# Local attention with the heads' pairs in the two halves of TensorE, a new order of the period, and turns in the probabilities' banks

## Chip, cores and metric

The kernel runs on one core of one Trainium2 chip. The metric is the device time in microseconds of one execution; the time given is the median of several. A core has TensorE (PE in the profile, PEld its weight loads), VectorE (DVE), ScalarE (ACT), GpSimd (POOL) and SyncE (SP), each with a queue of its own that runs in order; they meet at semaphores.

## What is computed

The whole reference is a chain of blocks (a state-space block, a mixture of experts, a windowed attention and a local-attention block of two layers). The change touches the last alone. Each of its two layers does, for 4096 tokens of 128 channels (16 sequences of 256):

```python
h = shift_token(x)
q, k, v = split(h @ wqkv)              # 8 heads of 64
q, k = rotary_xpos(l2norm(q) * qs, l2norm(k) * ksc)
sim = 8.0 * q @ k.T                    # windows of 64, each with the window before it
attn = softmax(where(mask, -max, sim))
x = x + (attn @ v) @ wo
x = x + feed_forward(layernorm(shift_token(x)))
```

## The kernel before

`phase_local` has one instruction stream for each engine, written out by hand. Each layer n has an attention stage of NB passes b, and each pass two chunks c = 0, 1 of 128 tokens. A number i = 2b + c counts chunks. Chunk 0 of a pass holds two windows whose keys lie in the same 128 tokens; chunk 1 also takes the 64 keys before each window. The 8 heads of a chunk are taken in two units u of four heads (HU = 4, U = 4 units in a pass).

The stages of a chunk, and who does them:

- `project` (L2620, PE): queries and keys into the two banks of `qk_ps`; `project_v` (L2625): values into the one bank `a_ps`.
- `rotary` (L3041 to L3043, DVE): three products with the tables, out of PSUM, into `c1` and `c2`. Their sum is made by DVE for keys (`rotary_sum`, L3048) and by POOL for queries (L2552).
- `square` (ACT, L2880) and `square_sums` (DVE, L3054); `query_norms` and `key_norms` (POOL, L2563 and L2573) take the power -1/2.
- `scale_k` (L3060, DVE) puts the norm into the keys; queries get theirs in the exponentials.
- `turn_q`, `turn_k` (L2633, L2641, PE): transposes, back into `qk_ps`; `q_copy` and `k_copy` (ACT, L2903) take them to SBUF. `kT` has two halves: in each only the 64 rows of one head of a pair are filled and the others stay zero, so that a product over all 128 rows gives one head. `qT` has both heads of a pair in its 128 rows.
- `scores` (PE): a bf16 product that writes the mask (L2654), then the products (L2658 for c = 0, L2663 for c = 1) on top of it, for one unit in one bank `s_ps[u % 2]`.
- `maxima` (DVE, L3070 and L3074): the row maxima and the exponentials' bias. `exps` (ACT, L2913): one instruction a head. `divide` (DVE, L3081 and L3084): the probabilities `pn`.
- `transpose_p` (PE, L2674) into `t_ps`, `p_copy` (ACT, L2922), `weigh` (PE, L2694 for c = 0, L2702 for c = 1) into `o_ps`, `o_copy` (ACT, L2928), `output` (PE, L2711) into `a_ps`, `residual` (DVE, L3090), which adds `a_ps` to the stream R.
- `transpose_r` (PE, L2612) turns R of a pass into `a_ps`, and `shift` (ACT) makes `hT` of it.

The functions `attend` of the four engines give the order of a pass: the chunks of pass b are scored while those of pass b + 1 are projected, and the last units of pass b - 1 are weighed. `first` and `last` leave out what the ends lack. `a_ps` is used in turn by output, the value projection and the transposes of R. After the attention stage come 8 groups of feed-forward.

Of the kernel before, what the change touches and what calls it, by code (L numbers as in the profile page):

```python
# [2419 lines left out]
def phase_local(nc, t, old, r_dram, x3_dram, out_dram):  # L2420
# [13 lines left out]
    with ExitStack() as ctx:  # L2434
# [8 lines left out]
        c1, c2 = ([m.sb(f"{n}{i}", [P, NH, HD]) for i in range(2)] for n in ("c1", "c2"))  # L2443
        qT = [m.sb(f"qT{i}", [P, NP, T]) for i in range(2)]
        kT = [m.sb(f"kT{i}", [P, 2, NP, T]) for i in range(2)]
        v = [m.sb(f"v{i}", [P, NCH, INNER]) for i in range(3)]
        near = [m.sb(f"near{i}", [P, INNER]) for i in range(2)]
        top, nbias = m.sb("top", [P, HU]), m.sb("nbias", [P, 2, HU])
# [21 lines left out]
        s_ps = [m.ps(f"s{i}") for i in range(2)]  # L2470
        t_ps = [m.ps(f"t{i}") for i in range(2)]
        ft_ps = qk_ps[:, Q, :]
        h_ps = s_ps + t_ps
# [10 lines left out]
        CLEARED = 5  # L2484
        near_in = m.sem("near_in")
        NW = 16 * len(t.sources)

        with nc.Block() as block:  # L2488
# [50 lines left out]
            def _(pool):  # L2539
# [5 lines left out]
                for i in range(2):  # L2545
                    nc.gpsimd.memset(kT[i][:, :, :, :], 0.0).then_inc(cleared, 1)

                def rotary_sum(l, b, c):

                    i = NCH * b + c  # L2550
                    pool.wait_ge(l.rot_rd[Q], i + 1)
                    nc.gpsimd.tensor_tensor(c1[Q][:, :, :], c1[Q][:, :, :], c2[Q][:, :, :], ALU.add).then_inc(l.sum_rd[Q], 1)  # L2552
# [30 lines left out]
                for n in range(2):  # L2583
                    for b in range(NB):
                        for c in range(NCH):
                            if b == 0:
                                key_norms(at[n], b, c)
                                rotary_sum(at[n], b, c)
                                query_norms(at[n], b, c)
                                if n == 0 and c == 0:  # L2590
                                    clear(pool, old)
                            else:
                                rotary_sum(at[n], b, c)
                                query_norms(at[n], b, c)
                                key_norms(at[n], b, c)
# [8 lines left out]
            def _(pe):  # L2604
# [10 lines left out]
                def project(n, b, c, x):  # L2615
# [3 lines left out]
                    at_least(pe, l.xT_sb[x], (x + 1) * i)  # L2619
# [8 lines left out]
                def turn_q(n, b, c):  # L2628
                    l, i = at[n], NCH * b + c
                    pe.wait_ge(l.sum_rd[Q], i + 1)  # L2630
                    pe.wait_ge(l.sq_rd[Q], i + 1)
                    for j in range(NP):
                        last = pe.transpose(qk_ps[:, Q, j * P:(j + 1) * P],  # L2633
                                            c1[Q][:, 2 * j:2 * j + 2, :].rearrange("p h d -> p (h d)"), ident[:, :])
                    last.then_inc(l.xT_mm[Q], 1)

                def turn_k(n, b, c):
                    l = at[n]
                    pe.wait_ge(l.kn_rd, NCH * b + c + 1)
                    for j in range(NP):  # L2640
                        last = pe.transpose(qk_ps[:, K, j * P:(j + 1) * P],  # L2641
                                            c1[K][:, 2 * j:2 * j + 2, :].rearrange("p h d -> p (h d)"), ident[:, :])
                    last.then_inc(l.xT_mm[K], 1)

                def scores(n, b, u):

                    l, p, c, d = at[n], b % 2, u // NU, u % NU
                    i = U * b + u
                    if d == 0:
                        pe.wait_ge(l.xT_sb[Q], NCH * b + c + 1)  # L2650
                        pe.wait_ge(l.xT_sb[K], 2 * (NCH * b + c + 1))
                    at_least(pe, l.ex_rd, HU * (i - 1))
                    bank = s_ps[u % 2][:, :].rearrange("p (h k) -> p h k", h=HU)
                    pe.matmul(bank, identb[:, :], mask[:, c, :, :], start=True, stop=False, skip_group_check=True)  # L2654
                    for k in range(2):
                        j = 2 * d + k
                        if c == 0:
                            last = pe.matmul(bank[:, 2 * k:2 * k + 2, :], qT[p][:, j, 0:P], kT[p][:, :, j, 0:P],  # L2658
                                             start=False, stop=True, skip_group_check=True)
                        else:  # L2660
                            for r in range(2):
                                q0 = P + r * HD
                                last = pe.matmul(bank[r * HD:(r + 1) * HD, 2 * k:2 * k + 2, :], qT[p][:, j, q0:q0 + HD],  # L2663
                                                 kT[p][:, :, j, q0 - HD:q0 + HD], start=False, stop=True, skip_group_check=True)
                    last.then_inc(l.s_mm, 1)

                def transpose_p(n, b, u):
# [4 lines left out]
                    at_least(pe, l.pT_sb, i - 1)  # L2672
                    for h in range(HU):
# [40 lines left out]
                def attend(n, b, first=False, last=0):  # L2714

                    l = at[n]
                    scores(n, b, 0)
                    if not first:
                        transpose_p(n, b - 1, U - 2)
                    if last < 2:  # L2720
                        project(n, b + 1, 0, Q)
                        if first:
                            pe.wait_ge(l.hT_sb, 2 * (b + 2))
                        else:
                            pe.wait_ge(l.res_rd, NCH * (b - 1))
                        project_v(n, b + 1, 0)
                    if not first:
                        weigh(n, b - 1, U - 2)

                    turn_k(n, b, 1)  # L2730
                    scores(n, b, 1)
                    if last < 2:
                        project(n, b + 1, 0, K)
                    if not first:
                        transpose_p(n, b - 1, U - 1)
                    if last < 2:
                        turn_q(n, b + 1, 0)
                    if not first:
                        if last < 2:
                            pe.wait_ge(l.v_sb, NCH * (b + 1) + 1)  # L2740
                        else:
                            pe.wait_ge(l.res_rd, NCH * (b - 1))
                        output(n, b - 1, 0)
                        weigh(n, b - 1, U - 1)

                    scores(n, b, 2)
                    transpose_p(n, b, 0)
                    if last < 2:
                        project(n, b + 1, 1, Q)
                        if first:  # L2750
                            pe.wait_ge(l.v_sb, NCH * (b + 1) + 1)
                        else:
                            pe.wait_ge(l.res_rd, NCH * (b - 1) + 1)
                        project_v(n, b + 1, 1)
                    weigh(n, b, 0)
                    if last < 1:
                        pe.wait_ge(l.v_sb, NCH * (b + 2))
                        transpose_r(n, b + 2)

                    if last < 2:  # L2760
                        turn_k(n, b + 1, 0)
                    scores(n, b, 3)
                    if last < 2:
                        project(n, b + 1, 1, K)
                    transpose_p(n, b, 1)
                    if last < 2:
                        turn_q(n, b + 1, 1)
                    if not first:
                        if last == 0:
                            pe.wait_ge(l.hT_sb, 2 * (b + 3))  # L2770
                        elif last == 1:
                            pe.wait_ge(l.v_sb, NCH * (b + 2))
                        else:
# [519 lines left out]
```

## Time and profile before

| | |
|---|---|
| median of 3 runs | 2178.75 us (2176.16 to 2181.96) |
| profiled execution, its own time | 2176.2 us |
| its span, first to last instruction | 2174.4 us |
| mean granted clock of TensorE | 0.929 |
| PE busy | 1781.2 us (82%) |
| DVE busy | 1635.1 us (75%) |
| ACT busy | 1271.2 us (58%) |
| POOL busy | 957.9 us (44%) |

The shares are means over the whole span. Of it, the local-attention block takes what lies behind 1297 us: an attention stage from there to 1649 us, feed-forward, and the same again for layer 2 from about 1730 to 2062 us. In the rows below, the three windows of layer 1 are its first pass, its 14 middle passes and its last pass up to the first feed-forward product. In a timeline, a start and the next start give what an instruction costs in a full queue; the duration is longer, since the end of one overlaps the next. An idle time in brackets is that before the instruction, with what ended it.

### The profile page before, as it was taken

The page shows a single profiled execution, that of the slowest core. Times are in us where ns is not written, and L with a number is a line of the kernel's source. Part 1 is how long each engine was busy: PE and PEld are TensorE (multiplying, and loading weights), DVE is VectorE, ACT ScalarE, POOL GpSimd, SP SyncE. Part 2 cuts the span into 40 slices and gives each one's busy share as a digit, 9 for nine tenths or more (in the row PEclk, how much of TensorE's full clock was granted, in tenths as well). Part 3 has the DMA queues.
Part 4 walks back from the last instruction along what each step waited for, and adds up shares of the span by engine and source line. Part 5 has one row for each costly group of instructions (what it writes and reads, how often), then busy time and mean ns, then how long its engine had stood idle before and what let it go on. Part 6 is the DMA issues. An engine that isn't in the chain of part 4 may idle for free. (4 is left out here: it accounts for less than half of the span.)

```text
span 2174.4 us, 36880 instructions
## 1 busy us (share of the span) xinstructions
PE 1781.2 (82%) x12448; PEld 976.1 (45%) x12448; DVE 1635.1 (75%) x3467; ACT 1271.2 (58%) x2737; POOL 957.9 (44%) x773
## 2 busy tenths in 40 slices
PE   5888898865889998859943757999998899999875
PEld 2333333332344444424423424655655556566543
DVE  5999999995577777622235767999986689999775
ACT  5777877740344444414434236888884388888721
POOL 5777887761012222223431245555550255555311
PEclk8999999996899999959976878999999999999997
DMA  5333333312111111114235140000001000000010
GB/s 150 110 111 119 122 108 116 93 49 81 39 37 36 41 36 44 31 41 133 65 105 165 52 137 15 16 21 16 11 16 23 13 16 21 16 16 11 15 42 23
DMA packets 107401, 125.47 MB, mean 58 GB/s; under 512 B 28804, under 2 KB 79151, under 8 KB 106224
## 3 DMA queue, kind: packets, MB, share of 16 engines
q1 hardware_dynamic: 103120, 115.07, 18.7%
q0 software_dynamic: 4096, 8.06, 1.1%
q8 instruction: 101, 1.65, 0.3%
q14 instruction: 84, 0.69, 0.1%
HBM read 71.60 MB, written 38.11 MB: 50 GB/s over the span
## 5 line engine op out<-in xcount | busy, mean ns | idle before, releaser
L394 POOL TENSOR_TENSOR m_bu<-m_dtu,m_brow 128x1024 f32<-128x1024 f32 x128 | 299.8, 2358 | 55.6 <-DVE m_hs L818 53.9
L818 DVE TENSOR_TENSOR_SCAN m_hs<-m_ps_da,m_bu 128x1024 f32<-128x1024 f32 x128 | 292.3, 2283 | 3.0 <-POOL m_bu L394 2.5
L1363 ACT ACTIVATE a_pt<-a_ps_s 128x1024 f32<-128x1024 f32 x128 | 131.1, 1024 | 226.7 <-PE a_ps_s L1141 226.7
L523 PE MATMUL m_ps_y_ps<-m_prod,m_ident 128*128 128x512 f32 x512 | 243.1, 597 | 0.0
L2913 ACT ACTIVATE l_pe<-l_ps_s,l_nbias,l_qs 128x128 f32<-128x128 f32 x512 | 227.9, 459 | 1.6
L1480 DVE TENSOR_REDUCE a_mpad<-a_ps_s 128x4 f32<-128x1024 f32 x128 | 156.9, 1226 | 92.3 <-PE a_ps_s L1133 91.1
L1133 PE MATMUL a_ps_s<-a_heads 32*128 32x256 f32 x1024 | 187.5, 446 | 43.6 <-DVE a_mpad L1480 28.5
L670 ACT ACTIVATE m_ps_da<-m_dt,m_a_neg 128x510 f32<-128x510 f32 x256 | 166.0, 681 | 74.3 <-DVE m_hs L818 73.4
L1141 PE MATMUL a_ps_s<-a_qm,a_heads 32*128 32x256 f32 x1024 | 184.7, 437 | 1.8 <-ACT a_pt L1363 1.4
L1067 POOL TENSOR_TENSOR a_rstd<-a_ve,a_mhalf 128x2 f32<-128x2 f32 x48 | 33.8, 705 | 303.0 <-DVE a_ve L1438 163.3
L828 DVE TENSOR_TENSOR m_prod<-m_hs,m_ps_c_ps 128x1024 f32<-128x1024 f32 x128 | 153.6, 1200 | 12.1 <-PE m_ps_c_ps L509 12.1
L2620 PE MATMUL l_ps_qk<-t_wqkv,l_hT 128*128 128x512 f32 x256 | 140.7, 634 | 9.4 <-ACT l_kT L2903 5.8
L523 PEld LDWEIGHTS m_ps_y_ps<-m_prod,m_ident 128*128 128x128 f32 x512 | 96.6, 192 | 108.7 <-issue 106.6
L3084 DVE TENSOR_TENSOR l_pn<-l_pe,l_ri 128x512 f32<-128x512 f32 x128 | 138.6, 1082 | 4.4
L1133 PEld LDWEIGHTS a_ps_s<-a_heads 32*128 32x128 f32 x1024 | 82.2, 193 | 129.6 <-PE a_ps_s L1141 60.1
L2552 POOL TENSOR_TENSOR l_c<-l_c 128x512 f32<-128x512 f32 x64 | 103.9, 1623 | 42.4 <-DVE l_c L3043 42.4
L3070 DVE TENSOR_REDUCE l_top<-l_ps_s 128x4 f32<-128x512 f32 x128 | 88.2, 689 | 35.9 <-PE l_ps_s L2658 23.8
L509 PE MATMUL m_ps_c_ps<-m_bc,m_sel 96*128 96x512 bf16 x128 | 49.1, 383 | 76.4 <-DVE m_prod L828 69.3
L3041 DVE TENSOR_TENSOR l_c<-l_ps_qk,t_tab 128x512 f32<-128x512 f32 x128 | 87.9, 686 | 29.9 <-PE l_ps_qk L2620 29.8
L2563 POOL TENSOR_TENSOR l_qs<-l_sc,l_mhalf 128x8 f32<-128x8 f32 x64 | 106.6, 1666 | 5.3
L2573 POOL TENSOR_TENSOR l_rink<-l_sc,l_mhalf 128x8 f32<-128x8 f32 x64 | 106.6, 1665 | 5.4
L2913 ACT ACTIVATION_READ_ACCUMULATOR l_pe<-l_ps_s,l_nbias,l_qs 128x1 f32 x512 | 105.0, 205 | 0.0
(339 smaller groups left out, 4252.1 us busy)
## 6 DMA issues: line engine op xcount, KB each, us to landing
m_brow<-state_rows SPq DMA_DIRECT2D x64, 512.0 KB, 4.3
slots<-m_void SPq DMA_DIRECT2D x16, 516.0 KB, 5.4
l_near<-l_v SPq DMA_DIRECT2D x64, 128.0 KB, 2.3
e_xs<-slots SPq DMA_DIRECT2D x16, 258.0 KB, 2.8
ys<-m_void SPq DMA_DIRECT2D x8, 512.0 KB, 5.3
qk<-a_qk SPq DMA_DIRECT2D x16, 256.0 KB, 2.0
a_heads<-qk SPq DMA_DIRECT2D x64, 64.0 KB
ew_w<-in_w SPq DMA_DIRECT2D x2, 2048.0 KB, 11.8
```

The costliest lines, as they stand in the source:

```text
L394: nc.gpsimd.tensor_tensor(bu[s % 4][:, :, :], dtu[p][:, :, :], b2, ALU.mult).then_inc(bu_rd, 1)
L523: last = pe.matmul(y_ps[:, h, :], ident[:, :], prod[d % 3][:, h, :], start=False, stop=(s == NS - 1))
L670: last = nc.scalar.activation(da[s % 2][:, h, :, 1:], dt[p][:, h, :, 1:], ACT.Exp, scale=a_neg[:, h, s:s + 1])
L818: dve.tensor_tensor_scan(hs[s % 4][:, :, :].rearrange("p h t -> p (h t)"), da[s % 2][:, :, :, :].rearrange("p h q t -> p (h q t)"), bu[s % ...
L828: dve.tensor_tensor(prod[d % 3][:, :, :], hs[s % 4][:, :, :], c2, ALU.mult).then_inc(prod_rd, 1)
L1133: last = pe.matmul(dst[:, j, :], qT[p][r, g, c * P:(c + 1) * P], kT[p][r, g, :], start=True, stop=True)
L1141: last = pe.matmul(s2[:, j, :], kT[p][r, g, c * P:(c + 1) * P], qm[p][r, g, :], start=True, stop=True)
L1363: nc.scalar.activation(pt[t % 2][:, :, :], s2[:, :, :], ACT.Exp).then_inc(exp_rd, 1)
L1480: dve.tensor_reduce(dst, src[:, :, :], AX.X, ALU.max, negate=True).then_inc(max_rd, 1)
L2620: pe.matmul(qk_ps[:, x, :], hT[b % 2][:, c * P:(c + 1) * P], t.wqkv[n][:, x * INNER:(x + 1) * INNER], start=True, stop=True).then_inc(l.x_ ...
L2913: nc.scalar.activation(pe_[u % 2][:, h, :], s_ps[u % 2][:, h * P:(h + 1) * P], ACT.Exp, bias=nbias[:, u % 2, h:h + 1], scale=qs[b % 2][:, ...
L3084: dve.tensor_tensor(pn[u % 2][:, :, :], pe_[u % 2][:, :, :], ri[:, :].unsqueeze(2).to_broadcast([P, HU, P]), ALU.mult).then_inc(l.pn_rd, 1)
```

## The change

1. *Scores.* `kT` loses its zero halves: it holds both heads of a pair in its 128 rows, like `qT`. A score product now contracts 64 rows, those of one head, r = 0 or 1. Heads with r = 0 write bank 0 of `s_ps`, those with r = 1 bank 1. All 8 heads of a chunk are scored at once; there is one set of two banks. Chunk 1 has products of 64 rows by 64 columns. `maxima` is one reduce over both banks, and `k_copy` one copy.
2. *Turns.* From chunk 2 (queries) or 1 (keys) on, `turn_q` and `turn_k` write into `t_ps[1]` and `t_ps[0]`, the banks of the transposed probabilities, with waits for their copies; `project` waits for the rotary and the squares of the chunk before. `c1` gets two buffers.
3. *Order.* The `attend` of each engine is now one body for a chunk. TensorE: scores; the turn of R (c = 1); probabilities; both projections; probabilities; output; weigh; turn_k; project_v; weigh; turn_q.
4. *GpSimd.* The sum of the queries' rotary waits for `kn_rd`, the scaling of the keys of the chunk before. The key norm comes ahead of the query norm. The memsets of `kT` go.

```diff
+        kept = {Q: 2, K: 1}
+
+        def turned(i, x):
+            return qk_ps[:, x, :] if i < kept[x] else t_ps[1 - x][:, :]
...
                 def rotary_sum(l, b, c):
 
                     i = NCH * b + c
                     pool.wait_ge(l.rot_rd[Q], i + 1)
+                    if i > 1:
+                        pool.wait_ge(l.kn_rd, i)
...
+                    for r in range(2):
+                        pe.matmul(bank[r], identb[:, :], mask[:, c, :, :], start=True, stop=False, skip_group_check=True)
+                    for j in range(NP):
                         if c == 0:
+                            for r in range(2):
+                                last = pe.matmul(bank[r][:, j, :], qT[p][side[r], j, 0:P], kT[p][side[r], j, 0:P],
+                                                 start=False, stop=True, skip_group_check=True)
                         else:
+                            for q in range(2):
+                                q0 = P + q * HD
+                                for r in range(2):
+                                    last = pe.matmul(bank[r][side[q], j, :], qT[p][side[r], j, q0:q0 + HD],
+                                                     kT[p][side[r], j, q0 - HD:q0 + HD], start=False, stop=True,
+                                                     skip_group_check=True)
```

The new order of TensorE and of VectorE:

```diff
                 def attend(n, b, first=False, last=0):
 
                     l = at[n]
+                    for c in range(NCH):
+                        scores(n, b, c)
+                        before = (b, 0) if c == 1 else (b - 1, 1)
+                        behind = not first or c == 1
+                        if c == 1 and last < 1:
+                            pe.wait_ge(l.v_sb, NCH * (b + 1) + 1)
+                            transpose_r(n, b + 2)
+                        if behind:
+                            transpose_p(n, before[0], NU * before[1])
                         if last < 2:
+                            project(n, b + 1, c, Q)
+                            project(n, b + 1, c, K)
+                        if behind:
+                            transpose_p(n, before[0], NU * before[1] + 1)
+                        if not first:
+                            if c == 0:
+                                pe.wait_ge(l.v_sb, NCH * (b + 1))
+                            elif last == 0:
+                                pe.wait_ge(l.hT_sb, 2 * (b + 3))
+                            elif last == 1:
+                                pe.wait_ge(l.v_sb, NCH * (b + 1) + 1)
+                            else:
+                                pe.wait_ge(l.res_rd, NCH * (b - 1) + 1)
+                            output(n, b - 1, c)
+                        if behind:
+                            weigh(n, before[0], NU * before[1])
+                        if c == 0:
+                            turn_k(n, b, 1)
+                        elif last < 2:
+                            turn_k(n, b + 1, 0)
+                        if last < 2:
+                            if not first:
+                                pe.wait_ge(l.res_rd, NCH * (b - 1) + c + 1)
+                            else:
+                                pe.wait_ge(l.hT_sb, 2 * (b + 2 + c))
+                            project_v(n, b + 1, c)
+                        if behind:
+                            weigh(n, before[0], NU * before[1] + 1)
+                        if last < 2:
+                            turn_q(n, b + 1, c)
...
                 def attend(n, b, first=False, last=0):
+                    for c in range(NCH):
+                        summed = (b, 1) if c == 0 and not first else (b + 1, 0) if c == 1 and last < 2 else None
+                        if summed:
+                            square_sums(n, *summed, K)
+                        maxima(n, b, c)
+                        if summed:
+                            square_sums(n, *summed, Q)
+                        if last < 2:
+                            rotary(n, b + 1, c, Q)
+                        if c == 0:
+                            scale_k(n, b, 1)
+                        elif last < 2:
+                            scale_k(n, b + 1, 0)
+                        else:
+                            norm_stats(n, 0)
+                        if last < 2:
+                            rotary(n, b + 1, c, K)
+                            rotary_sum(n, b + 1, c, K)
+                        divide(n, b, NU * c)
+                        if not first:
+                            residual(n, b - 1, c)
+                        divide(n, b, NU * c + 1)
```

ScalarE's order: shift (c = 1), p_copy, all exps of the chunk, p_copy, k_copy, both squares, v_copy, o_copy, q_copy.

## Rows read from the trace of the kernel before

**Rows 1.** Windows of layer 1: length, PE, PEld, DVE, ACT, POOL busy, clock, DMA.
```profile
1323.71:1343.14 19.43, 16.08 (x86) 8.59 (x86) 16.66 (x34) 15.26 (x46) 9.01 (x8) 1.00 0.06 14
1343.14:1627.49 284.35, 269.65 (x1932) 170.51 (x1930) 262.31 (x534) 246.39 (x727) 152.84 (x140) 1.00 0.07 16
1627.49:1648.98 21.49, 16.26 (x158) 12.18 (x156) 11.23 (x36) 14.46 (x48) 2.91 (x3) 0.92 0.04 10
```

**Rows 2.** VectorE's timeline in one pass: start us, duration us, engine, line.
```profile
1449.57 0.69 DVE L3070 TENSOR_REDUCE l_top<-l_ps_s 128x4 f32<-128x512 f32 x1 [0.15 <-PE l_ps_s L2658]
...
1450.38 0.69 DVE L3054 TENSOR_REDUCE l_ss<-l_sq 128x8 f32<-128x512 f32 x1
1450.98 0.68 DVE L3041 TENSOR_TENSOR l_c<-l_ps_qk,t_tab 128x512 f32<-128x512 f32 x1
...
1452.36 0.69 DVE L3048 TENSOR_TENSOR l_c<-l_c 128x512 f32<-128x512 f32 x1
1452.97 0.28 DVE L3090 TENSOR_TENSOR t_r<-l_ps_a,t_r 128x128 f32<-128x128 f32 x1
...
1453.98 0.68 DVE L3054 TENSOR_REDUCE l_ss<-l_sq 128x8 f32<-128x512 f32 x1
...
1456.05 0.69 DVE L3041 TENSOR_TENSOR l_c<-l_ps_qk,t_tab 128x512 f32<-128x512 f32 x1 [0.55 <-PE l_ps_qk L2620]
...
1457.32 0.68 DVE L3060 TENSOR_TENSOR l_c<-l_c,l_rink 128x512 f32<-128x512 f32 x1
...
1458.13 1.55 DVE L3084 TENSOR_TENSOR l_pn<-l_pe,l_ri 128x512 f32<-128x512 f32 x1
1459.99 0.69 DVE L3070 TENSOR_REDUCE l_top<-l_ps_s 128x4 f32<-128x512 f32 x1 [0.31 <-PE l_ps_s L2663]
```

**Rows 3.** TensorE's timeline in the same pass; the tile of the array behind MATMUL.
```profile
1452.55 0.34 PE L2702 MATMUL l_ps_o<-l_pT,l_near 128*64 128x64 f32 x4
...
1453.16 0.39 PE L2654 MATMUL l_ps_s<-t_mask,t_identb 128*128 128x512 bf16 x1
...
1454.99 1.02 PE L2620 MATMUL l_ps_qk<-t_wqkv,l_hT 128*128 128x512 f32 x2
1455.85 1.02 PE L2625 MATMUL l_ps_a<-t_wqkv,l_hT 128*128 128x512 f32 x2
1456.80 0.66 PE L2694 MATMUL l_ps_o<-l_pT,l_v 128*64 128x128 f32 x8
...
1458.06 0.66 PE L2641 MATMUL l_ps_qk<-t_ident,l_c 128*128 128x128 f32 x4
1458.55 0.38 PE L2654 MATMUL l_ps_s<-t_mask,t_identb 128*128 128x512 bf16 x1
1458.86 1.08 PE L2663 MATMUL l_ps_s<-l_kT,l_qT 128*64 128x256 f32 x8
```

**Rows 4.** GpSimd's timeline: a sum beside VectorE's scaling, and one beside other work.
```profile
1457.49 1.65 POOL L2552 TENSOR_TENSOR l_c<-l_c 128x512 f32<-128x512 f32 x1 [0.75 <-DVE l_c L3043]
...
1716.94 1.27 POOL L2552 TENSOR_TENSOR l_c<-l_c 128x512 f32<-128x512 f32 x1 [2.07 <-DVE l_c L3043]
```

**Rows 5.** TensorE's timeline in the windowed stage: products over 32 rows.
```profile
800.60 0.48 PE L1133 MATMUL a_ps_s<-a_heads 32*128 32x256 f32 x2
800.62 0.48 PE L1141 MATMUL a_ps_s<-a_qm,a_heads 32*128 32x256 f32 x2
```

**Rows 6.** One line's instructions: a reduce of 1024 elements, min/median/max ns.
```profile
L1480 DVE TENSOR_REDUCE a_mpad<-a_ps_s x128: 1218/1226/1227, 533.9 to 919.9; 128x4 f32<-128x1024 f32 x128
```

**Rows 7.** The page's part 5: the exponentials, busy us, mean ns, idle before.
```profile
L2913 ACT ACTIVATE l_pe<-l_ps_s,l_nbias,l_qs 128x128 f32<-128x128 f32 x512 | 227.9, 459 | 1.6
```

**Rows 8.** Windows where TensorE paused: columns as in the first group.
```profile
1627.60:1631.10 3.50, 1.44 (x22) 1.21 (x22) 2.12 (x5) 1.23 (x5) 1.91 (x2) 1.00 0.02 5
1631.10:1634.50 3.40, 3.40 (x13) 2.85 (x13) 0.94 (x3) 3.33 (x11) 0.00 (x0) 0.50 0.00 0
1651.60:1655.00 3.40, 1.94 (x6) 0.64 (x5) 2.93 (x14) 0.69 (x1) 1.11 (x1) 1.00 0.08 14
```

More of the change, by code:

```diff
@@ L2643, in turn_k, with scores @@
                     last.then_inc(l.xT_mm[K], 1)
[L2645 to L2656, printed above, removed]
+                def scores(n, b, c):
+                    l, p, i = at[n], b % 2, NCH * b + c
+                    pe.wait_ge(l.xT_sb[Q], i + 1)
+                    pe.wait_ge(l.xT_sb[K], i + 1)
+                    at_least(pe, l.ex_rd, NH * i)
+                    bank = [s_ps[:, r, :].rearrange("p (j t) -> p j t", j=NP) for r in range(2)]
+                    side = [slice(r * HD, (r + 1) * HD) for r in range(2)]
+                    for r in range(2):
+                        pe.matmul(bank[r], identb[:, :], mask[:, c, :, :], start=True, stop=False, skip_group_check=True)
+                    for j in range(NP):
@@ L2716, in attend @@
                     l = at[n]
[L2717 to L2738, printed above, removed]
-                        if last < 2:
[L2740 to L2773, printed above, removed]
-                            pe.wait_ge(l.res_rd, NCH * (b - 1) + 1)
-                        output(n, b - 1, 1)
@@ L2899, in k_copy @@
                     if c == 0:
[L2900 to L2904 removed]
+                        at_least(act, l.s_mm, NCH * (b - 1))
+                    nc.scalar.copy(kT[b % 2][:, :, c * P:(c + 1) * P],
+                                   turned(NCH * b + c, K).rearrange("p (j t) -> p j t", j=NP)).then_inc(l.xT_sb[K], 1)
                 def exps(n, b, u):
@@ L3092, in attend @@
                 def attend(n, b, first=False, last=0):
-                    if not first:
-                        divide(n, b - 1, U - 2)
-                        square_sums(n, b, 1, K)
-                    maxima(n, b, 0)
-                    if last < 2:
-                        rotary(n, b + 1, 0, Q)
-                    scale_k(n, b, 1)
-                    if not first:
-                        divide(n, b - 1, U - 1)
-                    maxima(n, b, 1)
-                    if last < 2:
-                        square_sums(n, b + 1, 0, Q)
-                        rotary(n, b + 1, 0, K)
-                        rotary_sum(n, b + 1, 0, K)
@@ L3108, in attend @@
-                    if not first:
-                        residual(n, b - 1, 0)
-                    divide(n, b, 0)
-                    if last < 2:
-                        square_sums(n, b + 1, 0, K)
-                    maxima(n, b, 2)
-                    if last < 2:
-                        rotary(n, b + 1, 1, Q)
-                        scale_k(n, b + 1, 0)
-                    else:
-                        norm_stats(n, 0)
-                    divide(n, b, 1)
-                    maxima(n, b, 3)
@@ L3123, in attend @@
-                    if last < 2:
-                        square_sums(n, b + 1, 1, Q)
-                        rotary(n, b + 1, 1, K)
-                        rotary_sum(n, b + 1, 1, K)
-                    if not first:
-                        residual(n, b - 1, 1)
+                    for c in range(NCH):
+                        summed = (b, 1) if c == 0 and not first else (b + 1, 0) if c == 1 and last < 2 else None
[4 more added lines that the diff above has]
+                            square_sums(n, *summed, Q)
+                        if last < 2:
+                            rotary(n, b + 1, c, Q)
+                        if c == 0:
+                            scale_k(n, b, 1)
+                        elif last < 2:
+                            scale_k(n, b + 1, 0)
+                        else:
+                            norm_stats(n, 0)
+                        if last < 2:
+                            rotary(n, b + 1, c, K)
[4 more added lines that the diff above has]
+                        divide(n, b, NU * c + 1)
```

147 lines of the change are left out of this document (66 added, 81 removed).

## Prediction

> **What bounds the kernel now.** I read the stage windows first. They cut layer 1's attention into its first pass (b = 0), the 14 middle passes and the last one [rows 1]: 284.35 us for 28 chunks of 128 tokens, 10.155 us a chunk, with TensorE busy 269.65 us (95%), VectorE 262.31 (92%), ScalarE 246.39 (87%) and the granted clock at 1.00. So three engines are nearly full, TensorE first, and no long wait is left; a change must shorten the work of both TensorE and VectorE to gain, and must not make them wait for each other. Layer 2 runs the same code and I take the same numbers for it.
>
> Then the timelines of VectorE [rows 2] and TensorE [rows 3] over one pass, for start-to-start costs (a duration overlaps the next instruction by about 0.09 us). The reader should see that VectorE's rows are back to back, and that there is one long L3084, 1.55 us instead of 0.69, which ends 0.54 us after GpSimd's sum at 1457.49 + 1.65 [rows 4].
>
> **What the change does to the work of a chunk.**
> - TensorE, scores. Before, a chunk of c = 0 is two units of four passes over 256 columns (0.86 each, as the two 512-column passes of a projection take [rows 3]), and one of c = 1 two units of 1.02. Now head pairs sit in the two 64-row halves of the array. That such row groups run side by side is shown by another stage: four matmuls on four groups of 32 rows start within 0.02 us [rows 5], where one after the other would start 0.21 apart (256 columns, half of a 512-column pass). [...] Per pair of chunks 3.8 becomes 2.0: 0.9 us less a chunk, and TensorE's 9.6 us becomes 8.7.
> - VectorE. Two maxima with their bias (0.81 each, 1449.57 to 1450.38) become one of 1024 elements. The same form takes 1.23 elsewhere [rows 6], so 1.35 with the bias: 0.27 less. GpSimd's sum now starts behind the scaling of the keys and lies beside the keys' rotary, which reads PSUM: the 0.87 of the long L3084 goes. 9.37 becomes 8.2.
> - ScalarE: one key copy over 128 partitions for two over 64. Eight exps remain, 8 x 0.46 = 3.7 us [rows 7]. It falls below 8.8 a chunk.
> - The turns now go to the probabilities' banks (`turned`), so a projection waits for the rotary and the squares of the chunk before and not for the copy of its turn. Both lie a slot back, so it has long been met and adds nothing.
> - The memsets of kT and their two signals only ran before the first chunk, beside loads and a projection on the slow clock: nothing.
>
> By work alone a chunk would cost 8.7 (TensorE) and not 10.155. But the orders are new, so I followed the waits around one chunk.
>
> **The loop that closes.** All of a_ps is one bank. Its users in a chunk i are the output of chunk i-2, the residual on VectorE that reads it, and then `project_v` of chunk i+2. In the new order `project_v` waits for that residual of the same slot, and VectorE's slot is: maxima, query sum of squares, rotary Q, scale_k, rotary K, its sum, divide, residual. Maxima waits for the scores of the slot. Behind `project_v` stand weigh and turn_q, then the next scores. So in every slot with a projection:
>
> scores -> maxima ... residual -> project_v -> weigh -> turn_q -> next scores.
>
> Its length, step by step:
> - scores to maxima: a first mask (one bf16 pass of 512 columns, half of an fp32 pass, 0.22), a second with the change of tile (0.31), matmul to maxima 1.13 (1458.86 to 1459.99), and 0.05 for a wider first weight load: 1.71 [rows 2, 3].
> - VectorE, maxima to residual: 1.35 + 0.60 (sum of squares, 1450.38 to 1450.98) + 1.27 (rotary Q, 1456.05 to 1457.32) + 0.60 (scale_k) + 1.38 (rotary K, 1450.98 to 1452.36) + 0.61 (its sum) + divide and residual 1.01 + 0.08 (one after the other, 1452.97 to 1453.98, and the end of the last) = 6.90 [rows 2].
> - the signal to TensorE: 0.06, estimated from the small gaps.
> - project_v 0.95, weigh 0.61, turn_q 0.49 (as turn_k, 1458.06 to 1458.55): 2.05 [rows 3].
>
> Sum 10.7 us (10.64 to 10.71 by chunk; I take 10.67), against 10.155. The residual used to be waited for one chunk later and so never closed a loop: now three engines have less to do and each chunk is 0.5 us longer. Over 28 chunks of two layers: 56 x 0.515 = +28.8 us.
>
> Other waits fit within it. The scores have one pair of banks now, so the next scores need all exps of the chunk: these end 1.4 + 3.7 us behind the start of maxima, and maxima to the next scores is 9.0. The last turn of probabilities (0.5), its copy (0.6) and the key copy follow them and are done by about 6.5. The key norm is ready before scale_k, since its sum of squares now comes before maxima. GpSimd's sum starts about 4.1 us behind maxima and takes 1.27 when nothing of VectorE disturbs it, 1.65 beside scale_k [rows 4]. At 1.27 it ends 5.4 behind; the keys' sum, held like that L3084 until 0.54 after it, then ends at 5.9, when it would anyway (5.20 + 0.69). At 1.65 it adds up to 0.4 to the loop (56 x 0.4 = +22). I take nothing, because the instructions beside it read PSUM.
>
> **The two ends.** In the first pass there is no residual to wait for. Its two slots are set by exps, key copy or pT copy, weigh and turn_q: about 8.2 us each, so 16 for 19.43 [rows 1], 3.4 less. The last pass has no projections: 1.4 + 3.7 + copy 0.6 + scores 1.7 = about 7.8 from scores to scores, then the last exps, one divide, norm, turns: about 17.4 for 21.49, 4.1 less. Two layers: -15 us, an estimate.
>
> Without any other effect: +28.8 - 15 = +14 us.
>
> **The clock.** TensorE now waits for the residual in each slot, 10.67 - 8.7 = 2 us, unevenly: about 2.2 in c = 0, 1.6 in c = 1, where the residual stream is transposed as well. [...] I expect falls in some slots: 12 in 56, with 0 and 28 (every c = 0) as bounds. A fall comes just as the wait ends, when all of TensorE's work is in the loop: 3.4 us at half speed lose up to 1.7; I take 1.6. 12 x 1.6 = +19 us; bounds 0 and +45.
>
> [...]
>
> [...]
>
> **Sum.** The profiled execution took 2176.2 us (span 2174.4, 1.8 around it), the median is 2178.75. 2176.2 + 14 + 19 = 2209; on the median 2212.
>
> **Rivals.**
> 1. *The work decides* (faster). If the loop had slack somewhere that I misread, a chunk falls to TensorE's 8.7: 56 x 1.45 = -81, with the ends -15: 2083. The point from which it decides is a loop under 10.4 us (below that the ends outweigh it). For it: all three engines lose work. Against it: every term of the 10.67 is a measured row and the waits are in the code.
> 2. *The loop without falls of the clock*: 2178.75 + 14 = 2193. It is the low side of my own case.
> 3. *The 64-row halves don't overlap*, or the small matmuls of c = 1 are issued too slowly: scores take another 0.9 to 1.7 us, all of it in the loop: 56 x 0.9 = +50 and more, 2262. Against it: rows 5, though those are 32-row groups. A fall in each c = 0 slot gives about 2238, and with GpSimd at 1.65 again 2260.
> 4. *The same*: a loop of 10.4, 0.27 shorter than mine, cancels the ends: 2179.
>
> **Chances.** The residual loop at about 10.7 with or without falls of the clock, 2187 to 2242: 0.66. Rival 3, 2242 to 2285: 0.16. Same (within 0.3%, 6.5 us, about what this measurement can tell from nothing): 0.08. Faster: 0.10. Range 2180 to 2262; the likeliest case alone 2187 to 2242. Slower 0.82.
>
> **What would show it.** Of the changed kernel: L3084 never long; one reduce of about 1.23 us a chunk; the pairs of score matmuls starting within 0.02 us; 28 middle chunks of about 10.7 us (300 us a layer, more with falls); TensorE and VectorE under 85% there; and as the longest wait of the stage `project_v` on the residual, about 2 us, 56 times. The granted clock under 1.00 in the middle would show the falls. I am wrong if the wait for the residual is short or absent, or if a chunk takes under 10.2 us.

## The result, and the profile after

| | before | changed |
|---|---|---|
| median of 4 runs, us | 2177.45 (2175.56 to 2181.96) | 2241.74 (2236.8 to 2242.72) |
| profiled execution, us (span) | 2176.2 (2174.4) | 2242.72 (2240.9) |
| mean granted clock | 0.929 | 0.913 |

The ratio is 1.0289, with a 95% interval of 1.0271 to 1.0307: 2.9% slower. The rise was 64 us where 33 was forecast.

The stage windows of layer 1 in the changed kernel, cut as in [rows 1] from first maxima to first maxima (length, PE, PEld, DVE, ACT, POOL busy, clock, DMA):

```profile
1324.97:1342.31 17.34, 13.35 (x107) 7.63 (x108) 15.55 (x32) 14.31 (x47) 6.87 (x8) 1.00 0.02 4
1342.31:1660.03 317.72, 258.60 (x2267) 171.19 (x2268) 229.19 (x477) 230.02 (x698) 142.86 (x141) 0.95 0.07 15
1660.03:1681.47 21.44, 15.42 (x170) 12.55 (x171) 10.51 (x30) 13.14 (x43) 3.28 (x3) 0.84 0.04 10
```

Against [rows 1], the 14 middle passes have less work on each engine (TensorE 259 us for 270, VectorE 229 for 262, ScalarE 230 for 246) and take 33.4 us longer; in the second layer the same stretch takes 32.8 us longer. Those 66 us are the whole difference: the first passes give back 4.9 (2.1 and 2.8), the last passes nothing (+0.1 for both), and all else is 5.1 longer.

What TensorE waits for, in the view of waits of layer 1's middle passes (us in total, times, longest):

```profile
PEld l_ps_a L2635 <- DVE t_r L3079: 65.7, 28, 2.7
PE l_ps_a L2635 <- DVE t_r L3079: 59.0, 28, 2.4
```

This is `project_v` (L2635) on the residual (L3079), in every one of the 28 chunks: 59 us of 318, which is all of TensorE's idle time there (317.72 - 258.60 = 59.1). The loop can be walked in the timelines of one chunk without a fall of the clock. First VectorE, from maxima to the next maxima (start, duration):

```profile
1410.39 1.23 DVE L3058 TENSOR_REDUCE l_top<-l_ps_s 128x8 f32<-128x1024 f32 x1 [4.08 <-PE l_ps_s L2672]
...
1415.57 0.71 DVE L3038 TENSOR_TENSOR l_c<-l_c 128x512 f32<-128x512 f32 x1
1416.20 0.17 DVE L3070 RECIPROCAL l_ri<-l_rs 128x4 f32<-128x4 f32 x1
1416.40 0.69 DVE L3073 TENSOR_TENSOR l_pn<-l_pe,l_ri 128x512 f32<-128x512 f32 x1
1417.01 0.28 DVE L3079 TENSOR_TENSOR t_r<-l_ps_a,t_r 128x128 f32<-128x128 f32 x1
...
1421.21 1.22 DVE L3058 TENSOR_REDUCE l_top<-l_ps_s 128x8 f32<-128x1024 f32 x1 [2.51 <-PE l_ps_s L2678]
```

And TensorE's timeline from the end of that residual to the scores:

```profile
1417.35 1.13 PE L2635 MATMUL l_ps_a<-t_wqkv,l_hT 128*128 128x512 f32 x2 [2.17 <-DVE t_r L3079]
1418.40 0.34 PE L2723 MATMUL l_ps_o<-l_pT,l_near 128*64 128x64 f32 x4
...
1419.02 0.66 PE L2645 MATMUL l_ps_t<-t_ident,l_c 128*128 128x128 f32 x4
1419.51 0.59 PE L2668 MATMUL l_ps_s<-t_mask,t_identb 128*128 128x512 bf16 x2
1420.04 1.10 PE L2678 MATMUL l_ps_s<-l_kT,l_qT 64*64 64x128 f32 x32
```

VectorE needs 6.90 us from maxima to the end of the residual, TensorE 3.92 from there to the next maxima, 10.82 in all, and each waits while the other works: TensorE 2.17 us, VectorE 2.51. The divide ahead of the residual costs 0.81 (reciprocal and product, 1416.20 to 1417.01).

The fall of the clock, in three windows of 3.40 us:

```profile
1403.10:1406.50 3.40, 1.55 (x10) 0.71 (x10) 3.10 (x8) 2.47 (x7) 0.34 (x2) 1.00 0.01 2
1406.50:1409.90 3.40, 3.40 (x22) 2.37 (x20) 0.00 (x0) 1.38 (x3) 1.80 (x2) 0.50 0.35 77
1409.90:1413.30 3.40, 3.40 (x24) 2.27 (x21) 2.88 (x6) 2.04 (x8) 0.72 (x2) 1.00 0.01 2
```

TensorE was busy for 1.55 of 3.40 us around a wait for the residual (2.00 us, ending at 1404.95); in the next 3.40 the granted clock was 0.50 instead of 1.00. VectorE has no work at all in that window: all that is left of the loop is TensorE's part, as the prediction said, so the half speed goes straight into the slot. Such a slot takes 12.36 to 12.40 us, the others 10.81 to 10.86. There are nine in each layer's middle. Of the 16 distances between them 12 are 34.1 us, which is near to three slots of which one is drawn out (10.83 + 10.83 + 12.40 = 34.06); the others are 23.9 or 44.4 us. In layer 1 two slots hold another 0.24 and 0.34 us (11.06 and 12.73), which nothing here explains. So the middles come out as 56 x (10.83 - 10.155) + 18 x 1.57 = 37.8 + 28.3 = 66.1 us, where 66.2 was measured.

### The profile page after: what moved, and what is told of

Read it like the earlier page. It is cut to its first block and busy times, and to the rows that moved or that the text cites. A ratio compares the mean times of both kernels' runs of the same rounds, so it can differ in the third digit from the quotient of the medians.

```text
span 2240.9 us, 38370 instructions
## 1 busy us (share of the span) xinstructions
PE 1757.5 (78%) x13216; PEld 979.1 (44%) x13216; DVE 1561.0 (70%) x3339; ACT 1233.3 (55%) x2673; POOL 931.1 (42%) x771
## 5 line engine op out<-in xcount | busy, mean ns | idle before, releaser
L3058 DVE TENSOR_REDUCE l_top<-l_ps_s 128x8 f32<-128x1024 f32 x64 | 78.4, 1225 | 190.8 <-PE l_ps_s L2672 100.2
L2635 PE MATMUL l_ps_a<-t_wqkv,l_hT 128*128 128x512 f32 x128 | 72.3, 647 | 117.7 <-DVE t_r L3079 117.7
L2630 PE MATMUL l_ps_qk<-t_wqkv,l_hT 128*128 128x512 f32 x256 | 125.0, 610 | 0.8 <-ACT l_hT L2875 0.8
L2922 ACT COPY l_pT<-l_ps_t 128x512 f32<-128x512 f32 x128 | 76.7, 599 | 64.0 <-PE l_ps_t L2695 63.2
L2576 POOL TENSOR_SCALAR l_sc<-l_ss 128x8 f32<-128x8 f32 x64 | 15.4, 241 | 210.8 <-DVE l_ss L3044 210.8
```

Of the source, the lines that this page charges most:

```text
L2630: pe.matmul(qk_ps[:, x, :], hT[b % 2][:, c * P:(c + 1) * P], t.wqkv[n][:, x * INNER:(x + 1) * INNER], start=True, stop=True).then_inc(l.x_ ...
```

## The experiments

The runs were made on three chips. On two of them the kernel before takes 2215.5 and 2216.0 us, some 38 more. In the traces from these two the first maxima of layer 1 come at 1360 to 1370 us, in the others at 1324 to 1328, so nearly all of the difference lies ahead of the local attention. So ratios to the kernel before on the same chip are compared, or the length of layer 1's and 2's middle passes.

**The place of the residual.** The diagnosis is a loop through VectorE's queue. If it is right, what stands ahead of the residual counts in full, although the amount of work is unchanged. The first run puts one divide behind the residual, the second the keys' rotary and its sum as well.

```diff
     rotary(n, b + 1, c, K)
     rotary_sum(n, b + 1, c, K)
+    residual(n, b - 1, c)
     divide(n, b, NU * c)
-    residual(n, b - 1, c)
     divide(n, b, NU * c + 1)
```

```diff
+    residual(n, b - 1, c)
     rotary(n, b + 1, c, K)
     rotary_sum(n, b + 1, c, K)
     divide(n, b, NU * c)
-    residual(n, b - 1, c)
     divide(n, b, NU * c + 1)
```

> The changed kernel with one edit: VectorE makes the residual ahead of the first divide instead of behind it. Theory (the residual loop sets the slot): the loop loses one divide, 0.81 us, so a middle chunk takes 10.02 instead of 10.83 us, TensorE's wait for the residual falls from 2.2 to about 1.4 us and the clock no longer falls in the middle: 2242 - 56 x 0.81 - 17 x 1.57 = about 2170 us. Rival (the slot is set by something else, such as TensorE's new order of turns and weighs): 10.83 us a chunk and 2242 us as before the edit.

> The changed kernel with one edit: VectorE makes the residual right behind the scaling of the keys, ahead of the keys' rotary. Theory: the loop through the residual falls to about 8.1 us and no longer binds; a chunk is set by TensorE's own work and by the loop scores, maxima, exps, copy of the probabilities, weigh, turn_q, both about 8.7 us. 2242 - 56 x 2.1 - 27 for the falls of the clock = about 2100 us, below the kernel before. Rival: 10.83 us a chunk as before, 2242 us; or VectorE now waits for the output there, since TensorE finishes it just about then, and gives back some tenths a chunk (2120 us).

Middle passes of layer 1, first of the one, then of the other:

```profile
1379.77:1660.75 280.98, 243.12 (x2239) 162.10 (x2268) 231.76 (x477) 229.91 (x698) 142.48 (x141) 1.00 0.08 17
```
```profile
1386.25:1635.53 249.28, 237.70 (x2239) 161.39 (x2268) 231.33 (x476) 221.59 (x698) 141.58 (x140) 1.00 0.08 19
```

With the residual ahead of the divide the ratio to before is 0.9952 [0.9935, 0.997], and a slot takes 10.02 us: the 0.81 of the divide, to the hundredth. The wait for the residual is 1.18 to 1.60 us, and no slot has a fall of the clock. Without falls the window also shows TensorE's own work in a chunk, 243.12 / 28 = 8.68 us, where 8.7 was forecast. With the residual ahead of the keys' rotary too, the ratio is 0.9654 [0.963, 0.9677] with slots of 8.81 and 9.00. The same instructions, one of 0.28 us in another place, take 249 instead of 318 us a layer. The loop is shown, and so is that it made the changed kernel slow, together with the falls of the clock that its wait brings. TensorE is now busy 95% of the time; its timeline shows what it still waits for (0.38 us, charged to no releaser), and ScalarE's shows two squares, of which the first, that of the queries, ends at 1508.67:

```profile
1507.73 0.66 PE L2715 MATMUL l_ps_o<-l_pT,l_v 128*64 128x128 f32 x8
1508.77 0.63 PE L2645 MATMUL l_ps_t<-t_ident,l_c 128*128 128x128 f32 x4 [0.38 <-issue]
```
```profile
1508.01 1.15 ACT L2881 ACTIVATE l_sq<-l_ps_qk 128x512 f32<-128x512 f32 x2
```

`turn_q` still waits for that square. The wait guarded the bank of `qk_ps` into which it turned before the change; it turns into a bank of the probabilities now and overwrites nothing that the square reads.

**The clock.** If the falls come from TensorE's pauses, then more work in the pause must make the kernel faster. The output product, which lies ahead of the wait and is not in the loop, is done three times (twice for nothing).

```diff
+  for _ in range(3):
       for j in range(NP):
           last = pe.matmul(a_ps[:, 0:C], oT[c][:, j, :], ...)
```

> The changed kernel with TensorE's output product made three times over into the same bank before it signals, which adds 1.7 us of matmuls a chunk with the same result. Theory (the clock falls because of TensorE's wait): the output ends at 5.4 us behind the start of maxima, before the residual at 6.6 needs it, so the loop stays 10.83 us; the wait shrinks from 2.2 to 0.5 us, no fall of the clock is left in the middle passes, and 17 x 1.57 = 27 us go: 2215 us, with twice the output's work more on TensorE. Rival (more TensorE work costs time, as the engine is the bound): 56 x 1.7 = +95 us, 2337 us. Second rival (falls have another cause): 2242 us with falls as before.

Its middle passes in layer 1, TensorE busy 293 us instead of 259:

```profile
1381.84:1685.72 303.88, 293.07 (x2687) 212.13 (x2716) 231.89 (x477) 229.20 (x698) 143.07 (x141) 1.00 0.07 16
```

The ratio is 1.0153 [1.0127, 1.0179] against 1.0289 for the changed kernel. The slot is still 10.83 us, the wait for the residual is 0.21 to 0.74 us, the clock is 1.00 throughout and no fall is left. The middles of both layers together are 27.7 us shorter than those of the changed kernel (18 x 1.57 = 28.3): that is what the falls cost in the middles, and it was won by adding work.

**The changed kernel again, and without the hold.** The first run repeats the changed kernel, the second takes the hold of GpSimd's query sum out of it.

```diff
     pool.wait_ge(l.rot_rd[Q], i + 1)
-    if i > 1:
-        pool.wait_ge(l.kn_rd, i)
```

> The changed kernel without an edit, so that it stands beside its variants on one chip. Theory: 28 middle chunks of 10.83 us a layer, plus 1.57 us for each fall of the clock, 16 to 19 falls; 2.9% above the kernel before. What would speak against the loop: middle chunks of another length on another chip.

> The changed kernel without GpSimd's wait for the scaling of the keys. Theory: in the new order GpSimd makes the query norm first and is free only 4.1 us behind the start of maxima, later than the scaling of the keys ends (3.9), so the wait holds nothing: same time within 0.3%, and the sums start where they did. Rival (the hold is what takes the 0.87 us of the long L3084 away): the long divides or a long scaling of the keys come back, and the slot grows by up to 0.87 us, +49 us.

The repeat has a ratio of 1.030 [1.0282, 1.0317], slots of 10.83 and 19 slots with a fall; without the hold it is 1.0299 [1.028, 1.0319], with the same slot. GpSimd's sum in layer 1 (count, min/median/max ns), with the hold and without:

```profile
L2558 POOL TENSOR_TENSOR l_c<-l_c x25: 1265/1282/1286, 1346.4 to 1619.2; 128x512 f32<-128x512 f32 x25
```
```profile
L2556 POOL TENSOR_TENSOR l_c<-l_c x24: 1276/1284/1290, 1347.7 to 1609.6; 128x512 f32<-128x512 f32 x24
```

Both start behind the query norm, which ends later than the scaling of the keys (at 1414.49 and 1414.27 in the chunk walked above). In the new order the hold does nothing.

**The hold in the old order.** The kernel before, with the same two lines added to its `rotary_sum`.

> The kernel before with GpSimd's wait for the scaling of the keys alone. Theory: in the old order the sum starts some 0.6 us later and beside the divide, so it takes 1.27 instead of 1.65 us, ends 0.2 us later, and the long divide behind it ends 0.2 us later too: no gain, ratio 1.000 to 1.005. Rival (the hold takes the 0.87 us of the long divide away): up to 28 us less, 0.987.

The ratio is 0.9996 [0.9979, 1.0013]. All divides of both layers, and the window of layer 1's middle (VectorE's busy time was 262.31 in [rows 1]):

```profile
L3086 DVE TENSOR_TENSOR l_pn<-l_pe,l_ri x128: 691/692/699, 1375.2 to 2102.1; 128x512 f32<-128x512 f32 x128
```
```profile
1386.22:1670.60 284.38, 266.79 (x1904) 170.39 (x1930) 238.23 (x533) 246.62 (x727) 157.28 (x140) 1.00 0.07 16
```

The long divide of [rows 2] is gone, VectorE has 24 us less to do, and the stretch takes 284.38 us where it took 284.35. In its timeline the 0.87 has become idle time in front of the maxima, waiting for TensorE's scores:

```profile
1501.22 0.69 DVE L3086 TENSOR_TENSOR l_pn<-l_pe,l_ri 128x512 f32<-128x512 f32 x1
...
1503.09 0.69 DVE L3072 TENSOR_REDUCE l_top<-l_ps_s 128x4 f32<-128x512 f32 x1 [1.17 <-PE l_ps_s L2665]
```

The time came out as expected, the way did not quite: GpSimd's sum now starts with the divide instead of ahead of it, and is itself the one that is drawn out, to 1.80 us:

```profile
1501.24 1.80 POOL L2554 TENSOR_TENSOR l_c<-l_c 128x512 f32<-128x512 f32 x1 [1.41 <-DVE l_c L3062]
```

**Do the 64-row halves overlap?** Two runs: the scores of c = 0 in the changed kernel with all passes of one half ahead of the other's, and (on the best order, below) the old score products over 128 rows with zeros in the keys.

```diff
-    for j in range(NP):
-        for r in range(2):
+    for r in range(2):
+        for j in range(NP):
             last = pe.matmul(bank[r][:, j, :], qT[p][side[r], j, 0:P], kT[p][side[r], j, 0:P], ...)
```

```diff
-    pe.matmul(bank[r][:, j, :], qT[p][side[r], j, 0:P], kT[p][side[r], j, 0:P], ...)
+    pe.matmul(bank[r][:, j, :], qT[p][:, j, 0:P], kT[p][:, r, j, 0:P], ...)
-    one key copy over 128 partitions, two buffers c1[Q]
+    two key copies over 64 partitions, one buffer c1[Q]
```

> The changed kernel with the score products of c = 0 in another order: four of the lower 64 rows, then four of the upper, instead of in turn. Same products, same banks. Theory (halves in turn run side by side, and scores lie in the loop): the scores of c = 0 stream for 1.71 instead of 0.86 us, 28 middle chunks become 0.86 us longer, 2242 + 24 = 2266 us, plus some more from the ends. Rival (the halves don't overlap in either order, or the engine sorts them itself): 2242 us.

> The fastest variant so far (residual ahead of the keys' rotary, turn_q without the square, copy between the exps) with the old way of the scores put back: the keys lie in two zero-padded halves, a product contracts all 128 rows, and the key copy is two instructions over 64 partitions again. The queries' rotary buffer is single again, to make room. Theory (in that order TensorE is the bound, and pairs of halves save stream time): scores stream 1.71 instead of about 1.0 us, a middle chunk takes about 9.2 instead of 8.48 us, +42 us: ratio 0.972 to the kernel before. So the contraction would be worth 40 us of the 100, and order and waits the rest. Rival (the order gives it all and the scores are hidden): 0.953 as that variant. Second rival (ScalarE, with 0.6 more, becomes the bound too): 0.98.

The 16 passes of a c = 0 chunk: as in the changed kernel (from the run with the residual ahead of the rotary), one half after the other, and over 128 rows:

```profile
1509.76 1.16 PE L2672 MATMUL l_ps_s<-l_kT,l_qT 64*128 64x128 f32 x16
```
```profile
1507.20 1.71 PE L2672 MATMUL l_ps_s<-l_kT,l_qT 64*128 64x128 f32 x16
```
```profile
1506.29 1.95 PE L2676 MATMUL l_ps_s<-l_kT,l_qT 128*128 128x128 f32 x16
```

So the halves run side by side: 1.16 us for 1.95. In the changed kernel each pass of one half starts within 0.01 us of one of the other half, as the prediction wanted it. Grouped, the passes start one by one, 0.11 us apart, except around the change of halves; so a part of the overlap is kept, which I had not expected (+0.54 measured in the c = 0 slot, 11.37 us, for 0.86 expected). The cost is in the loop. The ratio is 1.0455 [1.0426, 1.0484], since there are also more falls of the clock, some 28. Why there are more is open: the waits for the residual are no longer than in the changed kernel (1.65 to 2.40 us, 58.4 us a layer for 59.0). The grouped order loads weights into the same 64 rows eight times in a row; no run here separates the loads from the passes, so why it takes 1.71 us is not shown.

In the best order, where TensorE is the bound, the old way of the scores costs 22.7 us a layer in the middle passes (259.97 and 259.81 for 237.27 and 237.12), 0.81 a chunk. Layer 1's:

```profile
1378.26:1638.23 259.97, 255.33 (x2240) 185.66 (x2267) 232.69 (x476) 240.25 (x727) 141.76 (x141) 1.00 0.08 18
```

The ratio is 0.9791 [0.9763, 0.9819] instead of 0.953, so the new way is worth some 57 us of the 102 that the best order gains. That is more than the 0.972 expected, and the number of the second rival. The middles are 45 us longer (42 expected) and the first and last passes 8.5 us. ScalarE is busy 92% of the middle passes and TensorE 98%, so ScalarE is not shown to be a bound. The run also changes the key copy and a buffer, so the 57 us are not those of the products alone.

**How far the new order goes.** On the run with the residual ahead of the rotary: first `turn_q` without the wait for the square, except for the two first chunks, which still turn into `qk_ps`; then also ScalarE's second copy of probabilities between the exps.

```diff
-    pe.wait_ge(l.sq_rd[Q], i + 1)
+    if i < kept[Q]:
+        pe.wait_ge(l.sq_rd[Q], i + 1)
```

```diff
     exps(n, b, NU * c)
-    exps(n, b, NU * c + 1)
     if behind:
         p_copy(n, before[0], NU * before[1] + 1)
+    exps(n, b, NU * c + 1)
```

> The variant with the residual ahead of the keys' rotary, and in addition turn_q no longer waits for the square of the queries where it writes into the probabilities' bank (the wait guards a bank that it doesn't write there). Theory: turn_q starts at 1508.77 only when ScalarE's square has ended, 0.4 us behind the weigh; without it a middle chunk takes about 8.45 instead of 8.9 us, set by scores, maxima, exps, copy of the probabilities, weigh, turn_q: 25 us less than that variant (about 2.5 and 1.1 percentage points of the kernel before: ratio 0.954). Rival (the wait put down to issue is TensorE's own): ratio 0.965 as that variant.

> As the run before, and ScalarE's second copy of the probabilities goes between the two sets of exps. Theory: the second weigh no longer waits for it behind all eight exps, TensorE runs without a wait, and a chunk falls to TensorE's own 8.3 to 8.4 us; the last pass gains too, since its weigh no longer stands ahead of the last scores for a copy. Ratio to the kernel before 0.950. Rival: the copy delays the last exps by 0.5 us and with them the next scores; then 0.954, or worse.

The middle passes of the one and the other:

```profile
1344.10:1582.36 238.26, 238.09 (x2267) 161.36 (x2268) 230.30 (x477) 221.65 (x699) 141.45 (x140) 1.00 0.09 19
```
```profile
1343.50:1580.77 237.27, 237.18 (x2268) 161.37 (x2268) 229.62 (x478) 221.48 (x699) 141.17 (x140) 1.00 0.09 19
```

TensorE is busy for all but 0.2 and 0.1 us of the stretch. Slots are 8.43 and 8.58 (8.40 and 8.54). The ratios are 0.9538 [0.9522, 0.9554] and 0.953 [0.9514, 0.9546]; the second kernel takes 2078.04 us beside 2179.69 for the kernel before, 4.7% less, and 7.5% less than the changed kernel (0.953 / 1.030). It is the fastest of all. Their difference from each other lies within the intervals.

## Why the prediction was right, and where its sizes were off

Sign, mechanism and range were right; the size was not, 64 us for 33. Every term fell short in the same direction: the loop by 9 us, the falls of the clock by 9, the ends by 10, and 5 us no step had. That the result lies at the upper end of the likeliest case, 2242, is luck in part: that end was reached by allowing 28 falls, and 18 came. By the steps of the prediction:

- *The loop that closes.* Shown: the wait has the place, the count (56 times) and about the length forecast, and moving the residual ahead of one divide shortens the slot by exactly that divide. The term was 0.16 too small: 10.83 a slot, not 10.67, or 56 x 0.16 = 9 us. VectorE's part came out at 6.90 as added up, the signal at 0.06, mask to maxima at 1.70 for 1.71. Its 0.05 for a wider weight load was an estimate: in the kernel before, a load of 128x128 takes 0.19 us (L2658) and one of 128x64 0.14 (L2663). Two things make up the 0.16. `project_v` takes 1.05 to its successor (1417.35 to 1418.40) and not 0.95; that its first weight load, too, now waits for the residual with nothing to hide it (the PEld row of the waits) is my reading and was not tried alone. And the terms as the prediction wrote them add up to 10.72; taking 10.67 from its spread by chunks threw away the other 0.05.
- *The clock.* Shown by the run with more work. The number of falls was mis-sized, 18 instead of 12, their price of 1.6 was good (1.57): 28 us for 19. The 12 was the author's guess, and no run shows a rule that gives it. The wait in the c = 1 slots was mis-sized: 1.6 us were forecast and 2.00 came, against 2.17 for 2.2 in c = 0; falls followed waits of either kind. They came once in about three slots, for which no run shows the reason. With the loop shorter by 0.8 us (wait of 1.18 to 1.60) none came at all. Waits of 2.0 to 2.4 us brought them, and with waits of 0.21 to 0.74 in the run with three outputs they were gone.
- *The two ends.* -15 us were forecast and -4.8 came. The first passes gave 2.1 and 2.8, for 3.4 each: their two slots took 8.63 and 8.71 us (layer 1) and not 8.2. The last passes gave nothing instead of 4.1 each. The prediction's sum for them is wrong in itself (1.4 + 3.7 + 0.6 + 1.7 is 7.4 and not 7.8), yet its 7.8 "from scores to scores" was nearly met. Here is that part of layer 1's last pass and the part behind it in the changed kernel, then the first part in the run with three outputs, then the second in the run without the wait for the square (the cut is at the last maxima):

```profile
1660.03:1669.53 9.50, 7.02 (x87) 5.25 (x88) 4.53 (x9) 5.77 (x20) 2.27 (x2) 0.82 0.00 0
1669.53:1681.47 11.94, 8.40 (x84) 7.30 (x84) 5.98 (x21) 7.37 (x23) 1.01 (x1) 0.86 0.07 17
```
```profile
1685.71:1693.65 7.94, 7.02 (x102) 6.09 (x104) 4.53 (x9) 5.77 (x20) 2.38 (x3) 1.00 0.04 9
```
```profile
1591.62:1601.96 10.34, 7.05 (x84) 6.05 (x85) 5.97 (x21) 7.26 (x23) 1.01 (x1) 0.98 0.07 17
```

  At the full clock the two parts take 7.94 and about 10.3 us, 18.3 for the 17.4 forecast; each is 1.6 us longer with a fall of the clock in it. So two steps failed. The term for the falls left out the last passes, which have two falls (in [rows 8] the kernel before has one), and that costs 3.1 us here; and the work behind the last scores was put 0.7 us too low. The falls follow TensorE's longest waits, for ScalarE's second copy of probabilities, which stands behind all eight exps:

```profile
1665.65 0.34 PE L2723 MATMUL l_ps_o<-l_pT,l_near 128*64 128x64 f32 x4 [2.29 <-ACT l_pT L2922]
...
1675.15 0.66 PE L2715 MATMUL l_ps_o<-l_pT,l_v 128*64 128x128 f32 x8 [3.19 <-ACT l_pT L2922]
```

  The place of the copy in itself is worth little: with it between the exps the first part takes 7.83 us in layer 2, where it has no fall, for 7.94. The last passes then took 20.93 and 19.66 us, and without that move 19.61 and 21.45; in both runs the longer has two falls and the shorter one.
- *GpSimd's sum and the long L3084.* The lengths were right (1.28 us, no long divide), the cause was not: they go because of the new order, not because of the hold. Nor was the 0.87 worth anything where it stood, since it lay behind TensorE. It was no term of the time in the prediction, only of VectorE's load.
- *What the change does to the work of a chunk.* 8.7 us were forecast for TensorE's own work; the best version runs at 8.40 and 8.54. The 2.0 us for the scores of a pair of chunks take 1.02 for each, as the tiled products of a c = 1 unit took before (L2663, 1453.48 to 1454.50): 0.16 more than the 0.86 of the untiled ones, and no run shows what the 0.16 is made of. In the changed kernel the passes take 1.09 us from their first start to the next product's in c = 0 (1430.83 to 1431.92) and 1.03 in c = 1 (1420.04 to 1421.07). Rival 1 was therefore right about the work and wrong about the order in which it stood: it needed a loop under 10.4 us, and had one of 10.83. Its end at 2083 is near what the kernel with the order mended takes, 2078, but by another sum: the middle passes give 94 us for the 81 of the rival, the ends 10 for 15.
- *Rival 3*, halves that don't overlap, is ruled out by the two runs on it.
- The rest, +5 us outside the local attention's passes, no step had. Part of it may be the clock in the feed-forward that follows, where TensorE pauses for 2.93 us in the kernel before and for 2.92 in the changed one. Before, the clock stayed at 1.00 in the window behind that pause; in the changed kernel it did not:

```profile
1656.47:1659.90 3.43, 3.43 (x11) 1.83 (x12) 1.55 (x4) 1.62 (x3) 0.00 (x0) 1.00 0.19 46
```
```profile
1688.90:1692.30 3.40, 3.34 (x8) 1.69 (x9) 0.66 (x2) 1.47 (x2) 0.00 (x0) 0.63 0.18 46
```

## What to carry to other kernels

When a change makes three engines lighter, follow the waits once around a period before adding up the work: any bank with several users, written by one engine and freed by another in the same slot, closes a loop, and then every instruction that stands ahead of the freeing one in an in-order queue is paid in full, here 68 us in layer 1 for the place of one instruction of 0.28 us. Free first, compute later: an instruction that only releases a buffer belongs as far ahead in its queue as its data allow, and a wait that guarded a buffer goes when the buffer is another. And where the clock falls because of a pause that cannot be removed, useless work in the pause can pay for itself, here 27.7 us where it shortened waits of 2.0 to 2.4 us to 0.21 to 0.74.

## What the runs showed of the hardware that was not expected

- In the changed kernel's middle passes TensorE was busy for 81% of the time (258.60 of 317.72 us in layer 1), and still the granted clock fell nine times in the 28 slots of either layer, each time to 0.50 for 3.4 us. Waits of 2.0 to 2.4 us in every slot came with falls; waits of 1.18 to 1.60 in the run with the residual ahead of the divides, and of 0.21 to 0.74 in the one with three outputs, came with none. In the feed-forward, a pause of 2.93 us was followed by 1.00 in the kernel before, and one of 2.92 by a window of 0.63 in the changed one. So the length of the last pause does not tell by itself whether a fall comes, and no run shows what does.
- The order of passes in the two row halves matters: 1.16 us alternating, 1.71 grouped, for the same 16 passes. With the outputs split too, 32 passes in tiles of 64 by 64 take 1.10. A change of tile behind the mask came with 0.09 us: the product starts 0.31 us after the mask where it is tiled (the median of the changed kernel's 64 chunks), and 0.215 where it takes the whole array like the mask (c = 0 in the run with the old scores).
- GpSimd's sum of two tensors in SBUF and VectorE's product of two tensors in SBUF were drawn out beside each other, here the one that started later: the divide took 1.55 instead of 0.69 us when the sum was running ([rows 2, 4]), and the sum took 1.80 instead of 1.27 when it started 0.02 us behind the divide, which kept its 0.69. Beside VectorE's rotary products out of PSUM it takes 1.28 in the changed kernel (1414.44, 1265 to 1286 ns in layer 1).
